# A decoder of two layers on one core: value products between the first maxima's units, and stacks loaded in six transfers

## The chip, the core and the metric

The kernel runs on one core of a Trainium2 chip. The metric is the device time of one execution in microseconds (us). The engines are named as in the profile: PE is TensorE (its clock has two levels, 1.2 and 2.4 GHz; the profile gives the granted clock as 0.50 and 1.00), DVE is VectorE, ACT is ScalarE, POOL is GpSimd, SP is SyncE, which here only issues transfers (DMAs). PE writes to PSUM, which has eight banks of 128 x 512 f32.

## The reference

Six sublayers work one after the other on x, 2048 tokens x 256 channels, each followed by a residual sum and a layer norm:

```
x = layernorm(x + self_attention_with_rope(x))            # causal, 16 heads of 16
x = layernorm(x + cross_attention(x, ctx, mask))          # ctx 1601 x 256, a mask 2048 x 1601
x = layernorm(x + quantised_linear(x))                    # fp8
x = layernorm(x + gpt_block(x))                           # causal self attention, and an MLP 256-1024-256
x = layernorm(x + cross_attention(x, ctx))                # no mask
x = layernorm(x + mixture_of_experts(x))                  # 8 experts, the best two, and a shared one
# attention: softmax(q k^T * scale [+ mask]) v, by head
```

## The kernel before

Every sublayer is a stage with a block of code for each engine; semaphores order the engines inside it. `attention_phase` is used four times: stage 1 (causal, rope, 2048 keys), stage 2 (cross, masked, 1601 keys), stage 3 (causal, biases, the mask applied by POOL's select) and stage 4 (cross, no mask, biases). The change touches this function alone.

**The front.** The projections of q and k are made in 16 pieces, `work`, each 128 channels x 512 tokens (65 for the last piece of keys in a cross stage). PE makes a piece in one of four PSUM banks (`front_bank`, banks 3 to 6); ACT and DVE cut it into three bf16 parts: `cut_high` and `cut_middle` on ACT (L397, L403), `cut_rest` and `cut_low` on DVE (L633 or L636, L643). A buffer of `SLOTS` = 4 pieces holds the parts until `store` (L207) has sent them to DRAM (`q_parts`, `k_parts`); SP stores the even pieces and POOL the odd ones. `cut_high(i)` waits until store i - 4 has landed. ACT works in the order high(i), middle(i - 1); DVE in the order rest(i), low(i - 1). After the pieces PE makes the value tiles in the same four banks, 128 keys x 256 channels each (16 in a causal stage, 13 in a cross stage), as two products each, one for each half of the contraction (L465; the profile shows two instructions for each f32 product), and ACT copies a tile to `vall` (L418, semaphore `v_kept`).

**Stacks.** For head h the bf16 parts of q and k are gathered into one of three stacks, `ks[b]` and `qs[b]` with b = h % 3, of 96 rows (`load`, L240 and L241): the combinations of parts stand as six groups of 16 rows. The semaphore `stack_in[b]` counts the transfers. SP issues `load(0)` after store 10, `load(1)` after all stores, `load(2)` after the maxima of head 0, and `load(h + 2)` once the scores of head h - 1 are all made. All transfers of SP go through its one queue, in order. Three more rows of the stack (`KQ:KM`) take the negative maxima; the key side of them is set to 1.0 once in a stage (L738).

**Units.** `unit(h, u)` is a piece of the scores of head h for the row maxima: four PE products of 32 queries x up to 512 keys side by side (L492, on the diagonal L496 too) in banks 0 to 2, which DVE reduces (L659, with mask L655). A head has 40 units in a causal stage and 64 in a cross stage. PE may be three units ahead of DVE (`unit_used`). Head 0 has all its units before any score; then come the first units of head 1 (15, 19, 15 and 24 in the four stages). When head 0's units are reduced DVE makes the maxima in six steps (`finish_max`), SP sends them to DRAM and back into the stack (`place_max`, L250 and L253, semaphore `max_in`), and PE's first `scores(0, 0)` (L516) waits for that. From then on PE mixes scores, units of the next heads and products with the values (L544), ACT does the exponentials (L426).

Before the units, DVE sets constants: L738 for three stacks, L740 to L743 for the partial maxima, the ones among the values, and O_PS. POOL adds the bias to each value tile (L342, semaphore `v_shifted`) in stages 2 to 4, and in stage 1 it prepares the masks of stage 2 (L356 to L371) all along.

PE's queue before, after the pieces:

```
                for kind, i in front:
                    if loads and (kind, i) == front[len(work) if work[0][0][0] is None else 0]:
                        pe.wait_ge(loaded, 16 * len(loads))
                    made(kind, i)
                for u in range(nu):
                    unit(0, u)
                for u in range(early_units):
                    unit(1, u)
```

## Time and profile before

| | |
|---|---|
| median of 3 runs | 3175.15 us (3171.68 to 3175.83) |
| the profiled execution | 3167.93 us, its span 3165.9 us |
| PE busy | 2958.0 us, 93% of the span |
| DVE busy | 2265.6 us, 72% |
| ACT busy | 1730.3 us, 55% |
| stage 1 | 71 to 600 us |
| stage 2 | 600 to about 1400 us |
| stage 3 | about 1495 to 2000 us |
| stage 4 | about 2120 to 2800 us |

Busy time is the time in which an instruction of that engine runs. It doesn't tell which engine holds the others up: that is read from the waits in each stretch. The times of the rows are counted from the first instruction of the profiled execution.

### The profile page before, as it was taken

To read this page: it belongs to the slowest core of one execution; us is meant where nothing else is said; L and a number is where in the kernel's file an instruction comes from. 1 tells how busy PE (TensorE), PEld (TensorE's weight loads), DVE (VectorE), ACT (ScalarE), POOL (GpSimd) and SP (SyncE) were. 2 spreads that over 40 slices of the span, in tenths; PEclk is the share of its full clock that TensorE was granted. 3 is DMA by queue.
4 is the path that set the end of the run, shared out by engine and by line. 5 is a ranking of instruction groups with operands and counts; after the bars stand their busy time and mean duration, and the time that the engine had idled before them with its cause. 6 is when DMAs were issued, how large, how long until landed. Compare 5 with 4: busy or idle time off the path is not lost. (4 is left out here: it accounts for less than half of the span.)

```text
span 3165.9 us, 97114 instructions
## 1 busy us (share of the span) xinstructions
PE 2958.0 (93%) x41235; PEld 1694.2 (54%) x41235; DVE 2265.6 (72%) x5676; ACT 1730.3 (55%) x2207; POOL 502.0 (16%) x711
## 2 busy tenths in 40 slices
PE   5999999999999999995999999999999999989994
PEld 2566666545655566552466665563333333366662
DVE  6788888587777777747788886238999999551114
ACT  2366677525556556563377777332777777722220
POOL 0255565020000000000222212202000000001113
PEclk8899999979999999996899999997999999989998
DMA  2333333310001100100311111102012211121112
GB/s 72 115 105 107 109 109 91 115 41 24 23 15 24 25 23 17 29 25 27 102 39 39 39 41 47 63 20 85 24 51 67 59 52 32 36 86 44 45 40 77
DMA packets 129376, 172.62 MB, mean 55 GB/s; under 512 B 45199, under 2 KB 99087, under 8 KB 127343
## 3 DMA queue, kind: packets, MB, share of 16 engines
q1 hardware_dynamic: 112672, 119.09, 13.8%
q0 software_dynamic: 10800, 46.76, 4.6%
q8 instruction: 327, 5.36, 0.7%
q10 hardware_dynamic: 5472, 0.56, 0.1%
q14 instruction: 105, 0.86, 0.1%
HBM read 122.76 MB, written 35.16 MB: 50 GB/s over the span
## 5 line engine op out<-in xcount | busy, mean ns | idle before, releaser
L659 DVE TENSOR_REDUCE mpart<-ps 128x1 f32<-128x512 f32 (+5 forms) x2304 | 1242.7, 587 | 146.3 <-PE ps L492 76.1
L492 PE MATMUL ps<-stack 96*32 96x401 bf16 (+5 forms) x13312 | 1261.3, 354 | 9.7 <-DVE mpart L659 5.1
L516 PE MATMUL ps<-stack 99*32 99x512 bf16 (+3 forms) x11648 | 1135.5, 369 | 40.8 <-ACT xT L426 19.3
L426 ACT ACTIVATE xT<-ps 128x1024 f32<-128x1024 f32 (+3 forms) x800 | 732.0, 938 | 439.8 <-PE ps L516 240.6
L426 ACT ACTIVATE cn<-ps 128x1024 f32<-128x1024 f32 (+4 forms) x800 | 686.2, 870 | 314.8 <-PE ps L516 161.0
L492 PEld LDWEIGHTS ps<-stack 96*32 96x32 bf16 x13312 | 491.0, 96 | 497.8 <-DVE mpart L659 231.8
L655 DVE CUSTOM_DVE_ANT_0 scrap<-ps,arena 128x401 bf16<-128x401 f32 (+1 forms) x1024 | 550.2, 574 | 150.9 <-PE ps L492 126.7
L516 PEld LDWEIGHTS ps<-stack 99*32 99x32 bf16 x11648 | 412.6, 97 | 361.7 <-issue 121.3
L544 PE MATMUL ps<-xT,vall 128*17 128x512 f32 (+4 forms) x3648 | 454.9, 504 | 1.8 <-POOL xT L379 1.0
L544 PE MATMUL ps<-cn,vall 128*17 128x512 f32 (+3 forms) x3392 | 440.8, 495 | 1.7 <-ACT cn L426 0.9
L524 PE MATMUL ps<-arena,big 128*32 128x512 fp8e4 (+1 forms) x3264 | 359.6, 382 | 0.0
L496 PE MATMUL ps<-upper,ident 128*32 128x128 bf16 x2048 | 215.8, 226 | 0.0
L544 PEld LDWEIGHTS ps<-xT,vall 128*17 128x17 f32 (+1 forms) x3648 | 133.6, 98 | 50.9 <-issue 3.3
L524 PEld LDWEIGHTS ps<-arena,big 128*32 128x32 bf16 (+1 forms) x3264 | 120.8, 98 | 54.3 <-issue 5.3
L544 PEld LDWEIGHTS ps<-cn,vall 128*17 128x17 f32 (+1 forms) x3392 | 124.9, 97 | 44.7 <-ACT cn L426 3.5
L1492 PE MATMUL ps<-arena,vall 128*128 x312 | 146.6, 593 | 0.6 <-ACT vall L1563 0.6
L1722 DVE TENSOR_TENSOR vall<-osb,ps 128x512 f32<-128x512 f32 x39 | 26.8, 688 | 146.2 <-PE ps L1492 146.2
L521 PE MATMUL ps<-lower,ident 128*32 128x128 bf16 x1024 | 120.4, 222 | 0.4 <-issue 0.4
L496 PEld LDWEIGHTS ps<-upper,ident 128*32 128x32 bf16 x2048 | 105.1, 99 | 26.1 <-issue 1.1
L994 POOL PARTITION_ALL_REDUCE small<-small x1 | 0.4, 370 | 733.0 <-issue 733.0
L1577 ACT ACTIVATE osb<-ps 128x512 f32<-128x512 f32 x39 | 23.3, 597 | 169.8 <-PE ps L1492 169.8
L360 POOL TENSOR_SCALAR arena<-wbuf 128x401 bf16<-128x401 int32 x64 | 100.4, 1569 | 78.4 <-DMA wbuf<-in_mask 74.4
(258 smaller groups left out, 2573.4 us busy)
## 6 DMA issues: line engine op xcount, KB each, us to landing
stack<-q_parts SPq DMA_DIRECT2D x384, 64.0 KB, 2.5
wbuf<-in_mask POOLq DMA_DIRECT2D x16, 800.5 KB, 5.1
stack<-k_parts SPq DMA_DIRECT2D x192, 64.0 KB, 2.6
wbuf<-in_maskT POOLq DMA_DIRECT2D x12, 1024.0 KB, 5.2
arena<-in_moe_w SPq DMA_DIRECT2D x19, 512.0 KB, 4.1
stack<-k_parts SPq DMA_DIRECT2D x192, 50.0 KB, 2.2
stack<-sums_inverse SPq DMA_DIRECT2D x16, 512.0 KB, 6.2
parts<-osb SPq DMA_DIRECT2D x240, 32.0 KB
```

The lines of the kernel that those rows point to most:

```text
L360: chain.link(nc.gpsimd.tensor_scalar(e.mask_add[:, t, a:a + n], given[:, a:a + n], 0.0, MASKED, ALU.is_equal, ALU.mult))
L426: nc.scalar.activation(e.prob[tile % P_SLOTS][0:rows, half * HALF + first:(half + 1) * HALF], S_PS(g)[0:rows, first:HALF], ACT.Exp, scale= ...
L492: last = nc.tensor.matmul(bank[quarter(j), 0:w], qs[b][0:KQ, t * P + 32 * j:t * P + 32 * j + 32], ks[b][0:KQ, a:a + w], start=True, stop=n ...
L496: last = nc.tensor.matmul(bank[quarter(j), w - P:w], e.ident16[:, quarter(j)], e.upper16, start=False, stop=True)
L516: last = nc.tensor.matmul(S_PS(g)[quarter(j), lo:hi], ks[b][0:KM, kt * P + 32 * j:kt * P + 32 * j + 32], qs[b][0:KM, half * HALF + lo:half ...
L521: last = nc.tensor.matmul(S_PS(g)[quarter(j), lo:lo + P], e.ident16[:, quarter(j)], e.lower16, start=False, stop=True)
L524: last = nc.tensor.matmul(S_PS(g)[quarter(j), lo:hi], e.big16[0:rows, quarter(j)], e.mask_one[0:rows, kt, half * HALF + lo:half * HALF + h ...
L544: last = nc.tensor.matmul(O_PS[quarter(j, HD + 1), b0 * P:CH], e.values[0:rows, kt, h, :], weights[0:rows, b0:4, j, :], start=(kt == 0), s ...
L655: nc.vector.tensor_tensor_reduce(out=e.scrap[:, g % 4, 0:w], in0=src, in1=e.mask_add[:, t, a:a + w], scale=1.0, scalar=-3.0e38, op0=ALU.ad ...
L659: nc.vector.tensor_reduce(dst, src, AX, ALU.max).then_inc(unit_used, 1)
L1492: last = nc.tensor.matmul(bank, e.pair_xT[i % 2][:, c, :], w, start=(c == 0), stop=(c == NC - 1))
L1722: nc.vector.tensor_tensor(e.pair_h[i % 2], e.gated_s[i % 2], b_bank(i), ALU.mult).then_inc(pair_h, 1)
```

## The change

Five edits in `attention_phase`:

1. After the pieces PE makes the first eight value products (four tiles, one for each bank), and spreads the others (24 in a causal stage, 18 in a cross stage) evenly between the units of head 0 and the early units of head 1.
2. DVE's constants L740 to L743 move to the beginning of the stage. The three rows of ones (L738) move from DVE to POOL, behind POOL's stores and ahead of its bias work.
3. `load` has six transfers in place of twelve, for every head: groups of 48, 32 and 16 rows, for keys and for queries. The keys of a group are one array of 16 rows, read three times or twice.
4. `load(0)` goes out behind store 8, no longer behind store 10.
5. PE waits for the biased values (`v_shifted`) at the first product with the values, no longer before the first scores.

```
                     row = 0
                     for n in (3, 2, 1):
-                        for i in range(n):
-                            sp.dma_start(ks[b][row:row + HD, 0:keys], e.kd[h, :, 3 - n, 0:keys]).then_inc(stack_in[b], 16)
-                            sp.dma_start(qs[b][row:row + HD, :], e.qd[h, :, i, :]).then_inc(stack_in[b], 16)
-                            row += HD
+                        rows = slice(row, row + n * HD)
+                        sp.dma_start(ks[b][rows, 0:keys],
+                                     e.kd[h, :, 3 - n, 0:keys].unsqueeze(0).broadcast_to([n, HD, keys])).then_inc(stack_in[b], 16)
+                        sp.dma_start(qs[b][rows, :], e.qd[h, :, 0:n, :].rearrange("d s t -> s d t")).then_inc(stack_in[b], 16)
+                        row += n * HD
...
                 for i in range(0, len(work), 2):
                     store(sp, i)
-                    if i == n_first + 2:
+                    if i == n_first:
                         stored_until(sp, n_first)
                         load(0)
...
             def _(pool):
                 for i in range(1, len(work), 2):
                     store(pool, i)
+                for b in range(3):
+                    nc.gpsimd.memset(ks[b][KQ:KM, 0:keys], 1.0).then_inc(stack_set, 1)
+                pool.wait_ge(stack_set, 3)
                 pool.wait_ge(ahead_in, 16 * len(ahead))
...
+                def value_part(t, c):
+                    (a, n), bank = k_tiles[t], front_bank(("value", t))
+                    if c == 0:
+                        bank_free(place["value", t])
+                    part = nc.tensor.matmul(bank[0:n, 0:D], v_source[:, c, a:a + n], v_weights[:, c, :],
+                                            start=(c == 0), stop=(c == NC - 1))
+                    if c == NC - 1:
+                        part.then_inc(front_made, 1)
...
-                        pe.wait_ge(stack_in[b], 192 * (h // 3 + 1))
+                        pe.wait_ge(stack_in[b], 96 * (h // 3 + 1))
...
+                    if tile == 0 and v_bias:
+                        pe.wait_ge(v_shifted, nk)
...
-                for kind, i in front:
-                    if loads and (kind, i) == front[len(work) if work[0][0][0] is None else 0]:
-                        pe.wait_ge(loaded, 16 * len(loads))
-                    made(kind, i)
-                for u in range(nu):
-                    unit(0, u)
-                for u in range(early_units):
-                    unit(1, u)
+                turned_front = work[0][0][0] is None
...
+                for i in range(len(work)):
+                    made("cut", i)
...
+                valued, all_units, first_values = 0, nu + early_units, NC * FRONT
+                while valued < first_values:
+                    value_part(valued // NC, valued % NC)
+                    valued += 1
+                for u in range(all_units):
+                    unit(u // nu, u % nu)
+                    while valued < first_values + (NC * nk - first_values) * (u + 1) // all_units:
+                        value_part(valued // NC, valued % NC)
+                        valued += 1
                 pe.wait_ge(v_kept, nk)
-                if v_bias:
-                    pe.wait_ge(v_shifted, nk)
                 pe.wait_ge(rest_made, len(work))
```

On PE, at the end of stage 1's front, the last value tiles and the first units stood like this before (`wbuf,xT` are the value weights and the source, `stack` is head 0's stack, "32x512" one of the four products of a unit):

```order
L465 MATMUL ps<-wbuf,xT 128x256 [waits v_kept_239]
L465 MATMUL ps<-wbuf,xT 128x256
L492 MATMUL ps<-stack_240 32x128 [waits stack_in0_239]
L492 MATMUL ps<-stack_240 32x128 x3
L496 MATMUL ps<-upper,ident 32x128 x4
L492 MATMUL ps<-stack_240 32x256 x4
L496 MATMUL ps<-upper,ident 32x128 x4
L492 MATMUL ps<-stack_240 32x384 x4
```

and stand like this now, the value products being L485 and the units L501:

```order
L485 MATMUL ps<-wbuf,xT 128x256 [waits rest_made_239]
L485 MATMUL ps<-wbuf,xT 128x256
L501 MATMUL ps<-stack_240 32x128 [waits stack_in0_239]
L501 MATMUL ps<-stack_240 32x128 x3
L505 MATMUL ps<-upper,ident 32x128 x4
L501 MATMUL ps<-stack_240 32x256 x4
L505 MATMUL ps<-upper,ident 32x128 x4
L501 MATMUL ps<-stack_240 32x384 x4
L505 MATMUL ps<-upper,ident 32x128 x4
L485 MATMUL ps<-wbuf,xT 128x256 [waits v_kept_239]
L501 MATMUL ps<-stack_240 32x512 [waits unit_used_239]
L501 MATMUL ps<-stack_240 32x512 x3
```

The last value product ahead of the units is now one that waits for a piece to be cut (`rest_made`), and value products stand between the units.

On SP, in the same stage, store 10 and the first stack stood like this before (L207 is a store; "x2" are stores 8 and 10):

```order
L207 DMA q_parts<-parts 384x1x512 [waits low_239,middle_239,high_239] x2
L240 DMA stack_240<-k_parts 16x2048 [waits stored2_239,stored3_239,stored1_239,stored0_239]
L241 DMA stack_240<-q_parts 16x2048
L240 DMA stack_240<-k_parts 16x2048
L241 DMA stack_240<-q_parts 16x2048
```

and stand like this now:

```order
L207 DMA q_parts<-parts 384x1x512 [waits low_239,middle_239,high_239]
L240 DMA stack_240<-k_parts 48x1x2048 [waits stored2_239,stored3_239,stored1_239,stored0_239]
L242 DMA stack_240<-q_parts 48x1x2048
L240 DMA stack_240<-k_parts 32x1x2048
L242 DMA stack_240<-q_parts 32x1x2048
L240 DMA stack_240<-k_parts 16x2048
L242 DMA stack_240<-q_parts 16x2048
L207 DMA q_parts<-parts 384x1x512 [waits low_239,middle_239,high_239]
```

Store 10 now stands behind the six transfers of the first stack, in the same queue.

On DVE the last cuts and the first units of stage 1 stood like this before:

```order
L643 TENSOR_TENSOR parts<-parts 128x512 [waits middle_239] x2
L738 MEMSET stack_240 3x2048 x3
L740 MEMSET mpart 128x64 x2
L741 MEMSET vall 128x256
L742 MEMSET mneg 128x8
L743 MEMSET ps 128x512
L659 TENSOR_REDUCE mpart<-ps 128x1 [waits unit_ready_239,parts_set_239]
```

and stand like this now, with nothing between the two:

```order
L660 TENSOR_TENSOR parts<-parts 128x512 [waits middle_239] x2
L676 TENSOR_REDUCE mpart<-ps 128x1 [waits unit_ready_239,parts_set_239]
L676 TENSOR_REDUCE mpart<-ps 128x1 [waits unit_ready_239] x39
```

## Rows read from the trace of the kernel before

**Rows 1.** The page, busy time of each engine over the span.

```profile
PE 2958.0 (93%) x41235; PEld 1694.2 (54%) x41235; DVE 2265.6 (72%) x5676; ACT 1730.3 (55%) x2207; POOL 502.0 (16%) x711
```

**Rows 2.** Timeline, PE and DVE, stage 1: start, duration; in brackets the idle time before.

```profile
104.64 11.56 PE L465 MATMUL ps<-wbuf,xT 128*128 128x256 f32 x52 [0.65 <-DVE parts L633]
...
116.55 20.84 DVE L659 TENSOR_REDUCE mpart<-ps 128x1 f32<-128x128 f32 x40 [2.73 <-PE ps L496]
...
```

**Rows 3.** Timeline, DVE, the first reduction of units in stages 2, 3 and 4.

```profile
642.94 0.58 DVE L655 CUSTOM_DVE_ANT_0 scrap<-ps,arena 128x401 bf16<-128x401 f32 x1 [1.91 <-PE ps L492]
...
1538.47 1.68 DVE L659 TENSOR_REDUCE mpart<-ps 128x1 f32<-128x128 f32 x4 [4.15 <-PE ps L496]
...
2163.12 7.31 DVE L659 TENSOR_REDUCE mpart<-ps 128x1 f32<-128x401 f32 x15 [1.84 <-PE ps L492]
```

**Rows 4.** Windows: values, units at either clock, first scores; stages 1, 2, 3, 4.

```profile
core 0: us, PE busy (x) PEld busy (x) DVE busy (x) ACT busy (x) POOL busy (x), PEclk, DMA share, GB/s
...
116.10:121.90 5.80, 4.56 (x89) 1.62 (x88) 5.35 (x12) 1.67 (x2) 0.00 (x0) 1.00 0.26 71
121.90:144.80 22.90, 21.12 (x236) 5.39 (x233) 22.87 (x50) 0.00 (x0) 0.00 (x0) 0.50 0.03 7
144.80:152.60 7.80, 7.51 (x76) 2.67 (x80) 2.67 (x6) 3.88 (x4) 5.41 (x8) 0.50 0.33 93
...
683.70:688.50 4.80, 4.80 (x52) 1.81 (x52) 1.11 (x6) 2.05 (x2) 1.74 (x3) 0.50 0.36 96
...
1566.60:1572.50 5.90, 5.60 (x56) 2.04 (x60) 2.36 (x6) 3.86 (x4) 0.59 (x2) 0.50 0.45 120
...
2205.20:2210.80 5.60, 5.32 (x56) 1.88 (x56) 2.73 (x7) 3.41 (x4) 3.38 (x5) 0.50 0.15 36
```

**Rows 5.** Timeline, ACT: `cut_high` of pieces 11 and 14 of stage 1.

```profile
94.72 0.60 ACT L397 ACTIVATE parts<-ps 128x512 bf16<-128x512 f32 x1 [0.96 <-DMA k_parts<-parts]
...
100.00 0.60 ACT L397 ACTIVATE parts<-ps 128x512 bf16<-128x512 f32 x1 [0.53 <-DMA q_parts<-parts]
...
```

**Rows 6.** Timeline, ACT: `cut_high` of piece 11 in stages 2, 3 and 4.

```profile
624.21 0.69 ACT L397 ACTIVATE parts<-ps,bcol 128x512 bf16<-128x512 f32 x1 [0.20 <-DMA k_parts<-parts]
...
1514.35 0.69 ACT L397 ACTIVATE parts<-ps,bcol 128x512 bf16<-128x512 f32 x1 [0.69 <-DMA k_parts<-parts]
...
2144.34 0.69 ACT L397 ACTIVATE parts<-ps,bcol 128x512 bf16<-128x512 f32 x1 [0.29 <-DMA k_parts<-parts]
```

**Rows 7.** DMA view, 140.2 to 143.8 us: the maxima of head 0 are stored.

```profile
DMA packets 264, 0.02 MB, mean 5 GB/s; under 512 B 264, under 2 KB 264, under 8 KB 264
...
max_parts<-mturn SPq DMA_DIRECT2D x2, 8.0 KB
```

**Rows 8.** DMA view, 680.6 to 688.5 us: a load of maxima and twelve of a stack.

```profile
q1 hardware_dynamic: 390, 0.71, 34.1%
...
stack<-q_parts SPq DMA_DIRECT2D x6, 64.0 KB, 2.2
stack<-k_parts SPq DMA_DIRECT2D x6, 50.0 KB, 2.1
stack<-max_parts SPq DMA_DIRECT2D x1, 12.0 KB
```

**Rows 9.** Windows, 584 to 589 us: large loads on all 16 DMA engines.

```profile
584.00:589.00 5.00, 5.00 (x25) 4.36 (x24) 3.93 (x20) 3.93 (x10) 0.00 (x0) 1.00 0.97 384
```

**Rows 10.** Timeline, SP and PE, stage 3: a stack's first load, its first unit.

```profile
1593.40 0.32 SPq L240 DMA_DIRECT2D stack<-k_parts  x1
...
1610.79 0.23 PE L492 MATMUL ps<-stack 96*32 96x128 bf16 x3
```

**Rows 11.** DMA view, 165 to 195 us: POOL's mask transfers beside a stack (stage 1).

```profile
q0 software_dynamic: 288, 1.87, 17.3%
```

**Rows 12.** Groups by line: the DVE memsets of L738, a POOL elementwise group.

```profile
L738 DVE MEMSET stack<- x12: 1393/1579/1765, 106.5 to 2158.6; 3x2048 bf16 x6, 3x1601 bf16 x6
...
L369 POOL TENSOR_SCALAR wbuf<-wbuf 128x512 f32<-128x512 int32 x48 | 71.4, 1487 | 63.9 <-DMA wbuf<-in_maskT 60.8
```

More of the change, by code:

```diff
@@ L454, in _, with bank_free @@
             def _(pe):
-                def made(kind, i):
-                    f = place[kind, i]
+                def bank_free(f):
                     if f >= FRONT:
@@ L460, in made @@
                         pe.wait_ge(rest_made if held_by == "cut" else v_kept, which + 1)
+                def made(kind, i):
+                    bank_free(place[kind, i])
                     bank = front_bank((kind, i))
[L462 to L478 removed]
@@ L479, in made @@
-                    last.then_inc(front_made, 1)
+                    (w, bias, src), dst, o, a, n = work[i]
+                    if w is None:
+                        for t in range(n // P):
+                            at, place_of = bank[:, t * P:(t + 1) * P], a // P + t
+                            rows = slice(place_of * 2 * D + src * D + o * P, place_of * 2 * D + src * D + (o + 1) * P)
+                            nc.tensor.matmul(at, e.rot_own[:, rows], e.ident, start=True, stop=False)
+                            last = nc.tensor.matmul(at, e.rot_added[:, 2 * place_of + src, :], e.ident, start=False, stop=True)
+                    else:
+                        for c in range(NC):
+                            last = nc.tensor.matmul(bank[:, 0:n], w[:, c, o * P:(o + 1) * P],
+                                                    src[:, c, a:a + n], start=(c == 0), stop=(c == NC - 1))
@@ L729, in _ @@
                         nc.vector.memset(ks[b][:, keys:nk * P], 1.0).then_inc(pads_set, 1)
+                for m in e.mpart:
+                    nc.vector.memset(m, -3.0e38).then_inc(parts_set, 1)
+                nc.vector.memset(e.values[:, :, :, HD], 1.0).then_inc(parts_set, 1)
+                nc.vector.memset(e.mneg[:, 3 * NT:], 0.0)
+                nc.vector.memset(O_PS, 0.0).then_inc(parts_set, 1)
                 if loads:
@@ L736, in _ @@
                 cut_low(len(work) - 1)
-                for b in range(3):
-                    nc.vector.memset(ks[b][KQ:KM, 0:keys], 1.0).then_inc(stack_set, 1)
-                for m in e.mpart:
-                    nc.vector.memset(m, -3.0e38).then_inc(parts_set, 1)
-                nc.vector.memset(e.values[:, :, :, HD], 1.0).then_inc(parts_set, 1)
-                nc.vector.memset(e.mneg[:, 3 * NT:], 0.0)
-                nc.vector.memset(O_PS, 0.0).then_inc(parts_set, 1)
                 dve.wait_ge(parts_set, 4)
```

20 lines of the change are left out of this document (4 added, 16 removed).

## The prediction

> **What bounds the kernel now.** I read the page first: PE is busy 93% of the span, DVE 72% [rows 1]. That is an average over stages, so I went on to the timeline at the seams that the change touches. In stage 1 PE makes 26 value products in 11.56 us, 0.44 us each (two instructions for each f32 product), and only then come the units of head 0; DVE reduces its 40 units in 20.84 us, 0.52 us each, with nothing between them [rows 2]. So at a stage's beginning first PE works alone with the values, then DVE is the bound and PE waits for it. The windows give PE's clock there: granted 1.00 with the values and the first 5.8 us of the units, then 0.50 for 22.9 us of units, and it is still 0.50 for the first 7.8 us of scores, where PE is the bound (7.51 us busy). The same happens in the other stages: 4.8, 5.9 and 5.6 us of scores at 0.50, with 4.80, 5.60 and 5.32 us of PE work [rows 4]. From there on PE sets the pace.
>
> So the change can pay at two places: the values may hide beneath DVE's units, and the clock may be up when the scores begin.
>
> **The value products.** PE's work in units of full clock: a causal stage has 55 units, a cross stage 83 and 88. The columns of stage 1's 55 units, counted in the code, are 26,368, which is 11 us at 2.4 GHz; rows 4 give as an upper bound 21.12 / 2 + 4.56 = 15.1 us, values among them. DVE has 28 us beside it (55 x 0.52). The 24 moved products add 24 x 0.44 = 10.6 us: 21.5 us of 28 (at most 25.7), so at 1.00 DVE stays the bound and they are hidden. In a cross stage 18 products add 7.9 us to a PE that is otherwise busy about a third of the time: hidden too. By the columns PE then works three quarters of the stretch in stages 1 and 3 (before: 11 of 28, 39%) and half of it in stages 2 and 4 (before: a third). At 0.50 a unit with its product would take PE about 0.76 us in stages 1 and 3, above DVE's 0.52, and PE would be busy all the time. In the trace the clock fell only where PE waited for DVE, and no row here shows which of these shares holds it. I take it that it stays up in the causal stages, and comes back early or stays in the others.
>
> What that gives: the scores of rows 4 at full clock save half of 7.51 + 4.80 + 5.60 + 5.32 = 23.2 us, at most 11.6; I take **10.5**. Against it, the first eight products now run before the first units and after a PE that has waited, so some of them and the first units may be at 0.50: **2** lost. Behind the last early unit stand the last product, ACT's copy of that tile and a change of ACT's work before the first exponential, where before the tiles were long done: 0.4 us in stages 1 and 3, 1.5 in 2 and 4 (there a tile's last product falls on the last unit, which DVE ends later): **4** lost.
>
> **The first stack.** Whether the units start earlier depends on how long the stack takes. `load(0)` now stands behind the issue of store 8 and waits for stores 0 to 7 to land. `cut_high(11)` waits for store 7, so it marks that time: at 94.72 in stage 1 [rows 5], at 624.21, 1514.35 and 2144.34 in the others [rows 6]. Now the stack takes six transfers of 4 KB rows. How they are laid on the 16 DMA engines the rows tell by counting. The two small transfers of maxima in one window give 264 packets, that is 2 x (128 + 4): 128 data packets and 4 that complete it [rows 7]. That store has an outer dimension of 4, its other side one of 128. A stack of twelve transfers and the load of the maxima give 390 = 12 x (16 + 16) + (3 + 3): a 16-row transfer ends in 16 completions, a 3-row one in 3 [rows 8]. So a transfer uses as many engines as its outermost dimension has in common. The new transfers have an outer dimension of 3 (against 48) and 2 (against 32), the third pair 16: three engines, two engines, sixteen. Engine 0 carries 16 + 16 + 16 + 16 + 1 + 1 = 66 rows, 270 KB in stages 1 and 3, 241 KB in 2 and 4 (keys 3.2 KB), where before it carried 12 rows.
>
> The Trainium skill says the same, in "DMA: Bandwidth & Descriptors", section "Why a DMA increments its semaphore by 16 and not by 1": the number of engines is the largest up to 16 that divides the outermost dimension of both sides; its guidelines warn that a leading broadcast of c copies keeps the transfer on c engines. The packet counts of rows 7 and 8 agree with it. Had it 16 engines, the first rival below would be the sum.
>
> An engine's rate: large loads moved 384 GB/s at a share of 0.97 of 16 engines, 24.7 GB/s for one [rows 9]. So engine 0 needs **10.9 us** (9.8 in the cross stages). The upper end comes from the stack's own transfers: 34.1% of 16 engines in 7.9 us is 43.1 engine-us for 0.71 MB [rows 8], so 270 KB take 16.4 us (14.6). To either come about 2.3 us from issue to landing, which is what a 64 KB transfer of one row per engine takes (2.2) [rows 8]. I take the lower, since that is an engine that has work all the time, as engine 0 has here.
>
> Store 10 stands behind the stack in SP's queue, and its share of 24.6 KB on engine 0 comes last: with the two stores of POOL that share the engine, 3 x 1.0 us. It lands at 94.7 + 2.3 + 10.9 + 3.0 = 110.9 in stage 1, and `cut_high(14)` waits for it, which began at 100.00 before [rows 5]. **This is the wait that takes the place of the one removed**: the first value product followed `cut_high(14)` by 4.6 us [rows 2, 5], and the unit half a us later, so units start at 116.0 against 116.55: 0.5 gained [rows 2]. Stage 3: 1514.3 + 16.2 + 5.1 = 1535.6 against 1538.47, 2.9 gained. Stage 2: 624.2 + 15.1 + 4.6 = 643.9 against 642.94, 1.0 lost; stage 4: 2144.3 + 15.1 + 4.6 = 2164.0 against 2163.12, 0.9 lost [rows 3, 6]. Sum: **1.5 gained**. With the upper rate each stage is 4.8 to 5.5 us later: some 19 lost.
>
> **The later stacks.** In stage 3 the first transfer goes out at 1593.40 and the head's first unit comes at 1610.79 [rows 10]: 17.4 us of cover against 13.2 needed, 18.7 at the upper rate. The other heads of stages 1 and 3 have 17.4 to 18.7; those of the cross stages 26 to 37, enough at either. In stage 1 POOL's mask transfers take 17.3% of 30 us of all the engines [rows 11], some 2.3 us in 13: 15.5 against 17.5, still covered, 22 at the upper rate. Six issues less on SP are nothing on the path. I take **1** lost for shared engines.
>
> **The constants.** Each memset of L738 takes DVE 1.4 to 1.8 us, three in a stage [rows 12]; they stood in DVE's queue while PE made the values, so taking them away is worth nothing by itself, and is in the start already. On POOL the lower bound is the same 1.4 us; the upper a POOL elementwise group at 1.49 us for 512 columns [rows 12], four times that for 2048: 18 us for the three. POOL's last store goes by 116, and the first maxima come into the stack at about 143 [rows 7]: the lower bound is hidden with certainty, the upper with 9 us to spare, and I count nothing. If the cover were gone (in stages 2 to 4 the bias work stands behind them), the new wait at the first product with values, not the scores, would feel it. POOL's mask work of stage 1 starts as much later; stage 2 needs it 400 us on. Constants at a stage's beginning lie where DVE waits for pieces: nothing.
>
> **Sum.** 10.5 - 2 - 4 + 1.5 - 1 = 5 to 6.5 us (the 2 and the 4 overlap in part); I take 6.5 off 3167.93, 3161.4. The profiled execution lies 7.2 us below the median of the runs, so on their scale 3168.6: **3169**.
>
> **The rivals.**
>
> *All 16 engines carry the stack.* Then it takes 2.3 us and a few for the bytes, store 10 is not held up, and the units start when the cuts end: about 10.4 us (24 products of 0.44), 8, 11.5 and 8 us earlier in the four stages, 38 together; with the warm scores 11 and the tail -4 that is 45: 3128. For it: nothing in the diff forbids it. Against it: the counts of rows 7 and 8. Chance 0.12.
>
> *The clock is the loser (slower).* With PE waiting for the stack and then for DVE, the clock drops in the first units and stays at 0.50: a unit with its product takes PE 0.76 us in stages 1 and 3 against DVE's 0.52, 0.25 x 55 = 14 us each; in stages 2 and 4 about 1.5 each; no warm scores. 31 + 4 + 1 - 1.5 = 35 longer at the worst, about 3205 to 3212. Its point of decision: the clock at the first ten units. For it: 22.9 us at 0.50 in rows 4. Against it: PE would then be busy nearly without a break, which in this trace goes with 1.00 everywhere past the first scores. Chance 0.10.
>
> *The stack becomes a head's bound (slower).* At the upper rate a load needs 18.7 us in stage 3 and 22 in stage 1 against 17.4: up to 1.3 and 4.5 us for each of 13 heads, less what PE can draw from its other work, and the 19 lost at the starts. 10 to 60 longer, about 3195. It decides where 2.3 us and 270 KB take more than 17.4, that is below 18 GB/s for an engine. For it: rows 8's own rate. Chance 0.16.
>
> *Nothing to be seen or something else*, 0.05.
>
> **How the numbers follow.** Forecast 0.57, its own range 3158 to 3180 (warm clock kept in all stages or in none: +-8; start 5 us each way). The range from 3150 to 3200 leaves out the 16 engines (0.12) and the top of the two slow rivals. 0.2% is 6.3 us, about what a measurement of this kernel can tell from no change; the forecast stands just at this bound, so of its 0.57 about 0.27 is faster, 0.25 same, 0.05 slower. Faster: with the first rival 0.39, and 0.01. Slower: 0.05 + 0.08 + 0.12. Same: the rest.
>
> **What the profile would show.** PE's granted clock 1.00 at the first scores of stages 1 and 3. `cut_high(14)` of stage 1 starting near 111, released by a store of q; first unit near 116. The six transfers in the DMA view with 10 us and more from issue to landing, where twelve took 2.2. DVE's 40 units of head 0 still in 21 us, value products between them. The forecast is wrong if a unit waits for `stack_in` past 1610 in stage 3, if `cut_high(14)` starts near 100, or if the first ten units run at 0.50 with PE without a break.

## The result and the profile after

The changed kernel takes 3208.98 us (median of 4 runs, 3206.05 to 3218.43) against 3175.49 before: 1.0113 of the time, 95% interval 1.0100 to 1.0125. It is **slower by 1.1%**, where 3169 was forecast in a range up to 3200.

The profiled execution is the slowest of the four (3218.43), 50.5 us above that of before. So the account of the trace is larger than that of the medians (33.5 us). Three places in the trace tell what happened.

*The start.* ACT's timeline in stage 1 of the changed kernel, `cut_high` of pieces 11 to 14 [rows 5]:

```profile
96.10 0.60 ACT L401 ACTIVATE parts<-ps 128x512 bf16<-128x512 f32 x1 [0.57 <-DMA k_parts<-parts]
...
98.29 0.60 ACT L401 ACTIVATE parts<-ps 128x512 bf16<-128x512 f32 x1 [1.08 <-DMA q_parts<-parts]
...
105.52 0.60 ACT L401 ACTIVATE parts<-ps 128x512 bf16<-128x512 f32 x1 [6.12 <-DMA q_parts<-parts]
...
114.43 0.60 ACT L401 ACTIVATE parts<-ps 128x512 bf16<-128x512 f32 x1 [7.79 <-DMA q_parts<-parts]
```

Piece 14 waits 7.79 us for store 10 and goes at 114.43, where it went at 100.00; piece 13 has already waited 6.12 us, for store 9 on POOL's queue. A window just before piece 14 shows what is left to do (columns as in rows 4):

```profile
110.20:114.30 4.10, 0.00 (x0) 0.00 (x0) 0.00 (x0) 0.00 (x0) 0.00 (x0) 0.50 0.13 50
```

No engine computes, and the DMA share is 0.13 at 50 GB/s: two of sixteen engines work, at 25 GB/s each, and piece 14 waits for them. Then DVE, same stage [rows 2]:

```profile
120.04 1.24 DVE L676 TENSOR_REDUCE mpart<-ps 128x1 f32<-128x128 f32 x3 [1.71 <-PE ps L505]
121.73 8.56 DVE L676 TENSOR_REDUCE mpart<-ps 128x1 f32<-128x512 f32 x16 [0.46 <-PE ps L505]
130.45 12.10 DVE L676 TENSOR_REDUCE mpart<-ps 128x1 f32<-128x512 f32 x21 [0.16 <-PE ps L501]
```

The first reduction starts at 120.04 (116.55 before), though only eight of the 32 value products are still ahead of it.

*The clock.* Windows of the changed kernel: front of values, units and early units, first scores of stage 1; then units and scores of stages 2, 3 and 4 [rows 4]:

```profile
102.80:119.50 16.70, 6.88 (x19) 4.35 (x17) 4.47 (x7) 4.68 (x10) 1.32 (x2) 0.62 0.30 109
119.50:150.70 31.20, 30.57 (x373) 13.43 (x372) 29.54 (x61) 5.03 (x14) 5.41 (x4) 0.98 0.20 62
150.70:158.50 7.80, 6.57 (x124) 3.01 (x127) 4.52 (x8) 6.76 (x7) 5.35 (x8) 1.00 0.26 74
675.40:720.70 45.30, 39.74 (x369) 13.67 (x368) 42.52 (x172) 3.86 (x11) 11.31 (x15) 0.88 0.15 41
720.70:725.50 4.80, 4.79 (x56) 1.86 (x60) 0.00 (x0) 3.30 (x3) 2.43 (x4) 0.58 0.14 57
1574.10:1605.20 31.10, 30.47 (x373) 13.37 (x376) 29.49 (x61) 5.04 (x14) 15.24 (x20) 0.99 0.20 60
1605.20:1611.10 5.90, 4.61 (x84) 2.00 (x88) 2.70 (x5) 5.05 (x6) 1.27 (x3) 1.00 0.30 85
2206.10:2250.10 44.00, 37.76 (x389) 13.29 (x388) 43.45 (x94) 3.87 (x11) 11.29 (x15) 1.00 0.15 42
2250.10:2255.70 5.60, 4.31 (x72) 1.76 (x76) 2.38 (x5) 5.02 (x5) 3.92 (x6) 1.00 0.16 59
```

The granted clock is 1.00 or nearly so through the units of stages 1, 3 and 4 and at their first scores: that part came as forecast. PE is busy 30.6 of 31.2 us in stage 1, so the values just fill it. Stage 2 is the exception: 0.88 in the units and 0.58 at the first scores.

*The later heads of stage 1.* This is where most of the time went, and no row of the start tells it. What PE and SP waited for between 200 and 550 us, before and then after (group's line, releaser, us in total, times, longest):

```profile
PE ps L516 <- DMA stack<-max_parts: 4.1, 6, 1.5
...
SPq L253 <- DMA max_parts<-mturn: 24.5, 13, 3.2
```

```profile
PE ps L525 <- DMA stack<-max_parts: 19.6, 8, 3.3
...
PE ps L501 <- DMA stack<-q_parts: 2.0, 4, 0.8
...
SPq L254 <- DMA max_parts<-mturn: 37.0, 12, 4.9
```

The units wait for their stack in four heads, but only 2.0 us in all. PE's large wait is for the maxima, and their store takes 3.1 us (37.0 / 12) where it took 1.9. Eight of the twelve heads from head 3 on stand 28 to 32 us apart, where they stood about 27, and the clock drops to 0.50 behind these waits (30.7 us between the first and the last score of stage 1, before 14.6). From head 3's units to the last score, before and then after:

```profile
197.50:571.90 374.40, 360.56 (x7788) 250.63 (x7782) 303.20 (x612) 266.23 (x358) 203.83 (x178) 1.00 0.35 104
195.40:602.20 406.80, 373.54 (x7784) 256.39 (x7779) 306.10 (x612) 266.88 (x358) 210.19 (x182) 0.96 0.34 96
```

PE is busy 13.0 us longer, at a mean clock of 0.96, and idle 19.4 us longer: together 32.4 us.

Why the maxima are late is seen at single heads. From the issue of their store (L251) to the issue of their load back (L254), in the changed kernel, one head beside a mask transfer of POOL and one without:

```profile
256.94 1.19 SPq L251 DMA_DIRECT2D max_parts<-mturn  x2
257.31 0.60 POOL L360 DMA_DIRECT2D wbuf<-in_mask  x1 [0.30 <-POOL arena L375]
261.93 0.24 SPq L254 DMA_DIRECT2D stack<-max_parts  x1
...
341.81 1.19 SPq L251 DMA_DIRECT2D max_parts<-mturn  x2
344.40 0.24 SPq L254 DMA_DIRECT2D stack<-max_parts  x1
```

5.0 us against 2.6. The DMA view of 256.9 to 261.9 us (q0 is POOL's queue, q1 SP's):

```profile
q0 software_dynamic: 144, 0.82, 46.3%
q1 hardware_dynamic: 264, 0.02, 3.6%
```

SP's 264 packets are those of the two small stores alone [rows 7]: no stack is under way, and what the maxima wait for is POOL's mask. In eight heads of the changed kernel's stage 1 a mask transfer goes out between 1.0 us ahead of the store and 0.5 us behind it, and the store takes 4.9 to 6.2 us. In the kernel before none does: there the mask went out 1.4 to 3.6 us ahead in 13 heads, and the store took 2.5 to 4.3 us in all. The few engines of the stack come in one step earlier. The time to landing of POOL's `in_maskT` transfers, before and then after:

```profile
DMA to landing us min/median/max: 5.1/5.2/6.6
...
DMA to landing us min/median/max: 5.1/7.3/12.4
```

It is up to 12.4 us when the transfer goes out beside a stack. So POOL's round of two transfers and its arithmetic grows from 26 to 28 us to mostly 30 and more, longer than a head needs undisturbed (26.3), and the maxima's store keeps running into the next mask. That the rounds fall into step like this is read from the times; no run moved one against the other. Stage 3 has the same structure without POOL's mask transfers, and loses nothing there.

The account, from the starts of the same instructions in the two traces (us after less before):

| | stage 1 | 2 | 3 | 4 | sum |
|---|---|---|---|---|---|
| `cut_high(11)` to first unit | +2.0 | +3.4 | -0.3 | +4.2 | +9.3 |
| first unit to first score | +2.5 | +4.0 | +2.5 | +1.4 | +10.4 |
| first scores (stage 1: to head 3's units; others: to the last score) | -8.0 | -0.1 | -1.7 | -1.4 | -11.2 |
| stage 1, head 3's units to the last score | +32.4 | | | | +32.4 |
| up to piece 11 of each stage, and behind stage 4 | | | | | +8.6 |

Of the last line's 8.6 us, 6.1 lie behind the last score of stage 4, in code that is the same. The pieces 0 to 11, beside which the moved constants now stand, take as long as before in each stage, within 0.3 us.

### The profile page after: what moved, and what is told of

Same layout as the page of the kernel before. It is cut to its first block and busy times, and to the rows that moved or that the text cites. A ratio compares the mean times of both kernels' runs of the same rounds, so it can differ in the third digit from the quotient of the medians.

```text
span 3215.5 us, 96728 instructions
## 1 busy us (share of the span) xinstructions
PE 2942.3 (92%) x41234; PEld 1708.1 (53%) x41235; DVE 2251.7 (70%) x5664; ACT 1730.4 (54%) x2207; POOL 521.9 (16%) x723
## 3 DMA queue, kind: packets, MB, share of 16 engines
q1 hardware_dynamic: 103072, 119.05, 12.7%
## 5 line engine op out<-in xcount | busy, mean ns | idle before, releaser
L501 PE MATMUL ps<-stack 96*32 96x401 bf16 (+5 forms) x13312 | 1225.7, 343 | 14.0 <-DVE mpart L676 3.3
L525 PE MATMUL ps<-stack 99*32 99x512 bf16 (+3 forms) x11648 | 1142.0, 370 | 59.5 <-DMA stack<-max_parts 25.1
L501 PEld LDWEIGHTS ps<-stack 96*32 96x32 bf16 x13312 | 495.2, 96 | 465.5 <-DVE mpart L676 204.1
L525 PEld LDWEIGHTS ps<-stack 99*32 99x32 bf16 x11648 | 420.7, 97 | 375.8 <-issue 116.4
L364 POOL TENSOR_SCALAR arena<-wbuf 128x401 bf16<-128x401 int32 x64 | 100.5, 1570 | 102.2 <-DMA wbuf<-in_mask 98.3
```

The lines of the kernel that those rows point to most:

```text
L364: chain.link(nc.gpsimd.tensor_scalar(e.mask_add[:, t, a:a + n], given[:, a:a + n], 0.0, MASKED, ALU.is_equal, ALU.mult))
L501: last = nc.tensor.matmul(bank[quarter(j), 0:w], qs[b][0:KQ, t * P + 32 * j:t * P + 32 * j + 32], ks[b][0:KQ, a:a + w], start=True, stop=n ...
L525: last = nc.tensor.matmul(S_PS(g)[quarter(j), lo:hi], ks[b][0:KM, kt * P + 32 * j:kt * P + 32 * j + 32], qs[b][0:KM, half * HALF + lo:half ...
```

## The experiments

Theory 1: the transfers whose outermost dimension is 3 or 2 run on three or two DMA engines, which holds store 10 back at each start and, beside POOL's masks, the stacks and maxima of stage 1's heads. Theory 2: the loss lies in the values between the units, or in the place of `load(0)`. The runs form three groups, four rows of the table each, and each group has its own chip; the kernel before took 3152.77, 3167.62 and 3170.26 us there, so each ratio is to the kernel before on the same chip.

| run | median us (range) | to before (95%) |
|---|---|---|
| after_twelve | 3146.69 (3134.61 to 3164.97) | 0.9978 (0.9956 to 1.0000) |
| after_depth | 3135.78 (3121.23 to 3149.43) | 0.9950 (0.9931 to 0.9970) |
| before_six | 3216.74 (3216.10 to 3225.85) | 1.0204 (1.0187 to 1.0221) |
| after_store10 | 3209.06 (3185.45 to 3229.60) | 1.0155 (1.0115 to 1.0195) |
| before_again | 3167.00 (one run) | |
| first_depth | 3189.84 (3157.61 to 3197.17) | 1.0067 (1.0046 to 1.0088) |
| depth_values_ahead | 3176.40 (3171.93 to 3180.72) | 1.0026 (1.0016 to 1.0036) |
| depth_store10 | 3171.52 (3152.03 to 3174.07) | 1.0007 (0.9992 to 1.0022) |
| cross_ahead | 3159.70 (3144.70 to 3166.48) | 0.9955 (0.9938 to 0.9971) |
| cross_dense | 3143.21 (3134.93 to 3147.35) | 0.9910 (0.9894 to 0.9927) |
| after_thin_masks | 3185.81 (one run) | |
| depth_constants | 3204.51 (one run) | |

What the traces of these runs say of the places in question (us; "st." is the stage; the last column is the time from the first to the last score):

| kernel | cut 14, st. 1 | first unit, st. 1 | first unit to first score, st. 1 / 2 / 3 / 4 | scores, st. 1 |
|---|---|---|---|---|
| before | 100.0 | 116.1 | 28.7 / 41.3 / 28.6 / 42.6 | 427.1 |
| after | 114.4 | 119.5 | 31.2 / 45.3 / 31.1 / 44.0 | 451.5 |
| after_twelve | 105.8 | 110.7 | 30.7 / 45.8 / 30.8 / 58.9 | 427.2 |
| after_depth | 103.6 | 107.2 | 30.7 / 45.1 / 30.8 / 44.0 | 423.1 |
| before_six | 100.5 | 124.5 | 28.6 / 41.3 / 28.7 / 42.6 | 471.2 |
| after_store10 | 100.8 | 116.3 | 32.8 / 57.0 / 34.1 / 58.8 | 465.9 |
| before_again | 101.2 | 117.0 | 28.6 / 41.3 / 28.6 / 42.6 | 426.6 |
| first_depth | 102.8 | 106.4 | 30.7 / 45.1 / 31.7 / 44.1 | 441.3 |
| depth_values_ahead | 104.2 | 118.3 | 28.6 / 41.3 / 28.6 / 42.5 | 428.5 |
| depth_store10 | 100.3 | 107.0 | 30.7 / 56.9 / 35.9 / 58.7 | 419.1 |
| cross_ahead | 103.0 | 106.6 | 30.7 / 41.3 / 30.8 / 42.5 | 426.6 |
| cross_dense | 104.0 | 107.7 | 30.7 / 42.8 / 30.9 / 45.4 | 425.1 |
| after_thin_masks | 113.9 | 119.0 | 31.0 / 56.1 / 31.8 / 44.0 | 414.0 |
| depth_constants | 104.2 | 107.9 | 40.1 / 61.4 / 45.8 / 62.5 | 420.0 |

**after_twelve** puts the twelve transfers of 16 rows back into the changed kernel (and 192 for 96 in the wait).

> The changed kernel, but a stack in twelve transfers of 16 rows as before (all 16 engines by the completions). Theory 1, the few engines: store 10 is no longer held, cut_high(14) of stage 1 starts near 99 (114.43 in the changed kernel), the units start near 107, the heads of stage 1 go on at 27 us each; about 8 us gained at each of four starts, 11 for the warm first scores and the 30 of stage 1's heads back: 3125 to 3140. Theory 2, the values between the units or the order of queues cost the time: 3190 or more.

The gain over the changed kernel is there, 1.4% by the ratios, and the direction is theory 1's: units at 110.7, stage 1's heads back at 427.2. The size is not: 3125 to 3140 was expected, and `cut_high(14)` at 105.8 is still 5.8 us late, since SP issues the twelve transfers of the stack from 95.37 to 101.06 and store 10 only at 101.17. Stage 4 shows a new thing: 58.9 us from the first unit to the first score, all at 0.50. Its window, from the first unit on:

```profile
2149.90:2208.00 58.10, 57.50 (x385) 17.41 (x376) 44.70 (x94) 3.26 (x9) 10.79 (x15) 0.50 0.13 34
```

PE is busy 57.50 of 58.10 us: at half clock a unit with its share of the values takes longer than DVE needs. And the clock does not come back for it, though PE has hardly a pause.

**after_depth** keeps six transfers and changes only the order of the rows inside a group, so that the head's 16 dimensions are outermost on the DRAM side. Keys and queries are ordered alike, so the products are the same sums.

```diff
-e.kd[h, :, 3 - n, 0:keys].unsqueeze(0).broadcast_to([n, HD, keys])
+e.kd[h, :, 3 - n, 0:keys].unsqueeze(1).broadcast_to([HD, n, keys])
-e.qd[h, :, 0:n, :].rearrange("d s t -> s d t")
+e.qd[h, :, 0:n, :]
```

> The changed kernel with six transfers whose outermost dimension is the head's 16 dimensions on the DRAM side (row order inside a group: dimension, then part) and the 48, 32 or 16 rows of the stack on the other. Theory 1: 16 divides both, 16 engines carry them, so as with twelve transfers, 3120 to 3140. Theory 2 (six transfers are slow for their size, not for their outermost dimension, or the loss is elsewhere): about 3205.

3135.78, 0.9950: faster than before by 0.5%, and 1.6% below the changed kernel by the ratios, for the same bytes in the same six transfers. This is the run that isolates the outermost dimension.

The Trainium skill's rule in "DMA: Bandwidth & Descriptors", section "Why a DMA increments its semaphore by 16 and not by 1", gives 16 engines for 16 against 48, 32 or 16 rows. The trace agrees: in stage 3, from 1595.4 to 1599.0 us with a stack under way, the DMA share is 0.93 at 190 GB/s, and the transfers of 192 KB land in 3.6 and 4.0 us. The cuts in its stage 1:

```profile
102.07 0.60 ACT L401 ACTIVATE parts<-ps 128x512 bf16<-128x512 f32 x1 [3.31 <-DMA q_parts<-parts]
...
103.58 0.60 ACT L401 ACTIVATE parts<-ps 128x512 bf16<-128x512 f32 x1 [0.40 <-DMA q_parts<-parts]
```

Piece 14 goes at 103.58, and the first unit at 107.2, 12 us before the changed kernel's. Its clock through the units of stages 1, 2 and 4:

```profile
107.20:137.90 30.70, 30.09 (x369) 13.22 (x368) 29.66 (x62) 5.29 (x16) 6.01 (x4) 1.00 0.31 82
623.60:668.70 45.10, 38.85 (x373) 13.59 (x372) 42.53 (x172) 3.89 (x11) 12.34 (x16) 0.90 0.24 55
2132.00:2176.00 44.00, 37.78 (x393) 13.33 (x396) 43.43 (x94) 3.95 (x11) 12.12 (x16) 1.00 0.23 55
```

**before_six** has the six transfers of the change in the kernel before, and nothing else.

> The kernel before with nothing but the six transfers of the change. Theory 1: stage 1's heads 1.5 to 2.5 us longer each, since a stack lands 19 us after its issue beside the masks' transfers, and each start 2 to 5 us later: 3205 to 3225. Theory 2: 3170 to 3180.

1.0204: the six transfers alone cost more than the whole change did. First unit of stage 1 at 124.5, 8.4 us late; first to last score of stage 1 471.2 against 427.1. The unit does not wait for the stack itself. With the stack behind store 10, the next victim is store 11 on POOL's queue: piece 15 waits 7.07 us for it, the values start that much later, and they end only with the first unit.

```profile
108.70 0.60 ACT L398 ACTIVATE parts<-ps 128x512 bf16<-128x512 f32 x1 [7.07 <-DMA q_parts<-parts]
...
110.08 14.51 PE L466 MATMUL ps<-wbuf,xT 128*128 128x256 f32 x52 [5.22 <-DVE parts L634]
```

Theory 2 has nothing to say here, as values and order are those of before. In stage 1's heads PE waited 35.9 us for maxima and for no stack. The `in_mask` transfers, which now go out beside the stack, land in 8.5 us in the median (5.1 before), and 14 of the 16 stores of the maxima take 5.0 us and more:

```profile
wbuf<-in_mask POOLq DMA_DIRECT2D x16, 800.5 KB, 8.5
```

**after_store10** moves `load(0)` behind store 10 in the changed kernel.

```diff
-                    if i == n_first:
+                    if i == n_first + 2:
```

> The changed kernel with load(0) behind store 10 again. If only the few engines matter, the units wait for the stack itself in place of store 10: starts within 3 us of the changed kernel, 3200 to 3215. If the place ahead of store 10 is what costs, cut_high(14) is back near 100 and the units follow it: 3175 to 3190.

The ratio, 1.0155, is no better than the changed kernel's 1.0113, as theory 1 has it. `cut_high(14)` is back at 100.8, but the units start at 116.3, 3.2 us ahead of the changed kernel's: piece 15 now waits 7.26 us for store 11, and the first unit 3.66 us for its stack. The trace loses more elsewhere: the units and first scores of stages 2 and 4 ran at 0.50, and stage 1's heads took 465.9 us.

**before_again** is the kernel before, for a trace from the second chip.

> The kernel before, unchanged, for a trace from the chip on which these runs are made. Either theory: the milestones of stages 1 to 4 as in the first trace (slast of stage 4 within 10 us), and if the chip differs, a shorter time behind stage 4 (about 394 us, as in the other runs, where the first trace has 409).

Its milestones lie within 3.4 us of the first trace's in all four stages. The time behind stage 4 is 410.6 us, as in the first trace (409.5); the 394 us were of the chip of the first four runs. So the tail differs by 15 us between chips, and only ratios on one chip are compared here.

**first_depth** gives the first stack alone the 16 engines (`if h == 0`).

> The changed kernel, in which the first stack alone goes on 16 engines (rows ordered by dimension, then part); the stacks of heads 1 to 15 go as in the changed kernel. Theory 1 (two separate losses by the few engines: store 10 held at the starts, and stage 1's heads beside the masks): starts as in the run with 16 engines (units of stage 1 at 107 to 110, cut_high(14) below 106), and stage 1 from its first score to its last 450 us and more, against 423 with 16 engines: 3155 to 3170 on this chip. Rival: the loss in stage 1's heads follows from the late start alone; then 3136.

The two losses are separate: the starts are those of after_depth (units at 106.4), while stage 1's heads take 441.3 us against 423.1. The trace's 18 us are less than the 27 expected, but the trace is of the fastest of its five runs (3157.61); the median lies 32 us higher, at 1.0067, and what the longer runs spent it on no trace shows.

**depth_values_ahead** is after_depth with all value products ahead of the units (`first_values = NC * nk`).

> Stacks on 16 engines as in the run with the rows ordered by dimension, load(0) behind store 8, but all value products ahead of the units, as before the change. Theory A (values between units pay): about 10 us later units in stages 1 and 3, clock 0.50 for 20 us in each stage's units and in the first scores; some 15 to 25 us slower than with values between, 3150 to 3160. Theory B (what they save the clock takes back: units and values at 0.50 hold each other up in stages 2 and 4, 57 us for 44): runs spread by less than 10 us, and the median within 10 us of 3136.

Slower than the kernel before by 0.26%, and 0.8% above after_depth by the ratios: theory A. The spread is small, 9 us, as theory B had it. So both hold: values between the units pay on the whole (0.8%), and the spread is smaller without them. The units start at 118.3, later than before, although the stack was there long since: without this edit an early stack is worth nothing, as the values then set the start.

**depth_store10** is after_depth with `load(0)` behind store 10.

> As the run with the rows ordered by dimension, but load(0) behind store 10 (edit 4 undone). If edit 4 helps once the stack has 16 engines: the first unit waits for the stack, 3 us later in each stage, 12 us in all: 3148. If the cuts set the start: within 4 us of 3136.

First unit of stage 1 at 107.0 against 107.2: the place of `load(0)` changes nothing at this start (from piece 11 to the first unit, the other stages differ by -1.1 to +1.6 us). The run is 0.6% above after_depth all the same; in its trace both cross stages fell into the half clock. The windows of stage 4, the values ahead and then the units:

```profile
2136.00:2145.80 9.80, 6.86 (x26) 3.88 (x25) 5.38 (x10) 5.37 (x12) 1.66 (x3) 1.00 0.91 275
2145.80:2204.50 58.70, 57.71 (x393) 17.63 (x393) 44.72 (x94) 3.92 (x12) 12.87 (x16) 0.50 0.16 38
```

The clock was 1.00 when the units began, and fell with them. In the profiles with `load(0)` behind store 10 this happened in four of four cross stages, with it behind store 8, the constants early and the values spread over all units in two of ten. Whether the place has a part in that, or chance, stays open.

**cross_ahead** keeps the values between the units in the causal stages only (`NC * (FRONT if nu == 40 else nk)`).

> Stacks on 16 engines, load(0) behind store 8, and values between the units in the causal stages only; in the cross stages all value products stand ahead of the units. Theory B (in the cross stages units and values at 0.50 hold each other up, 57 us for 44, in some runs; in the causal stages the values between keep the clock at 1.00): first unit to first score 41.3 us in stages 2 and 4 in every run, 30.7 in 1 and 3; 0.7% below the kernel before, with a spread under 10 us. If the spread came from elsewhere (stage 1's heads, the chip), it stays at 25 us and more.

The stretches came as expected, 30.7 / 41.3 / 30.8 / 42.5, and the ratio is 0.9955, where 0.993 was expected. The spread is 22 us, 9 without the two fastest of nine runs: not under 10, so the cross stages were not its only source.

**cross_dense** has one value product after every second unit in the cross stages, until all are made.

```diff
+                spread = all_units if nu == 40 else 2 * (NC * nk - first_values)
-                    while valued < first_values + (NC * nk - first_values) * (u + 1) // all_units:
+                    while valued < first_values + (NC * nk - first_values) * min(u + 1, spread) // spread:
```

> As the run before it, but in the cross stages one value product after every second unit, so that the 18 are done after 36 units. If PE's share of the stretch decides on its clock: 1.00 through these 36 units, then 0.50 with DVE as the bound, 42 us from first unit to first score; 0.9% below the kernel before, spread under 12 us. If the clock falls at the first units all the same: 50 us and more from first unit to first score in stages 2 and 4 in some runs, and a spread of 20 us.

**The fastest: 0.9910 (0.9894 to 0.9927)**, with a spread of 12 us, about as the first of the two expectations has it. The windows of stage 4, the units with values and those without:

```profile
2132.10:2154.00 21.90, 21.57 (x201) 7.96 (x200) 20.23 (x39) 5.01 (x11) 11.92 (x16) 0.96 0.29 65
2154.00:2177.50 23.50, 21.98 (x196) 5.31 (x196) 23.46 (x54) 0.11 (x1) 0.00 (x0) 0.58 0.14 32
```

With a product to every second unit PE is busy 21.57 of 21.90 us at 0.96; the clock falls behind the last product, when DVE is the bound (busy 23.46 of 23.50 us). The two stretches, 42.8 and 45.4 us, are still 1.5 and 2.8 us longer than before the change. Against cross_ahead, on the same chip, the gain is in the start: from piece 11 to the first unit 12.7 and 13.5 us in stages 2 and 4, where it was 20.7 and 22.1. Against after_depth the traces show no gain in the stretches (45.1 and 44.0 there); that its median ratio is 0.4% lower comes from runs without a trace.

**after_thin_masks** leaves POOL's mask transfers of stage 1 in number, but cuts all except the first two to 8 columns; the masks are then all open, so stage 2 computes without its mask.

> The changed kernel, in which POOL's mask transfers of stage 1 but the first two bring 8 columns in place of 1601 and 2048; the masks then are all open, so stage 2 computes without its mask. POOL's arithmetic, the order and the number of transfers stay. Theory 1 (few engines beside the masks' traffic): stage 1 from first to last score 420 to 427 us (451.5 in the changed kernel), first scores still at 150 since store 10 is still held. Rival (the stacks on few engines are too slow by themselves): 440 and more.

Stage 1 from first to last score: 414.0, against 451.5. SP's and PE's waits between 200 and 550 us:

```profile
SPq L254 <- DMA max_parts<-mturn: 20.3, 14, 1.9
...
PE ps L527 <- DMA stack<-max_parts: 0.6, 2, 0.3
```

The store of the maxima takes 1.5 us (20.3 / 14), and PE waits for them 0.6 us and for a stack not at all. The stacks still go on few engines here. Beside after_depth (423.1) this says that the loss in stage 1's heads needs both: few engines, and POOL's megabytes. How much the kernel before would gain by thin masks was not run; it had 4.1 us of such waits. This is a single run, and it also shows stage 2 at half clock (56.1 us).

**depth_constants** is after_depth with the constants and the rows of ones set by DVE behind the last cut.

> Stacks on 16 engines, load(0) behind store 8, values between units, but the constants and the three rows of ones set by DVE behind the last cut, as before (edit 2 undone). Their 8 us on DVE then lie between the last cut and the first reduction: with the values no longer ahead of the units, first reduction 5 to 8 us later in each stage than with edit 2 (stage 1: 113 to 115 against 107.6), 20 to 30 us in all, unless the cuts' end was not the last wait.

DVE's timeline in its stage 1:

```profile
108.61 1.76 DVE L752 MEMSET stack<- 3x2048 bf16 x1 [0.48 <-issue]
110.75 1.76 DVE L752 MEMSET stack<- 3x2048 bf16 x1 [0.38 <-issue]
112.89 1.76 DVE L752 MEMSET stack<- 3x2048 bf16 x1 [0.38 <-issue]
114.73 0.19 DVE L754 MEMSET mpart<- 128x64 f32 x2
115.10 0.27 DVE L755 MEMSET vall<- 128x256 f32 x1 [0.19 <-issue]
115.31 0.07 DVE L756 MEMSET mneg<- 128x8 uint32 x1
115.49 0.48 DVE L757 MEMSET ps<- 128x512 f32 x1
116.00 1.09 DVE L673 TENSOR_REDUCE mpart<-ps 128x1 f32<-128x128 f32 x3
```

The first reduction starts at 116.00; with edit 2 it started at 107.63. So the constants cost 8.4 us in stage 1 once the values are no longer their cover; 5 to 8 was expected. PE, which waits through them, then has the clock at 0.50 for 10 to 62 us of each stretch; the single run's 3204.51 holds both.

## Why the prediction was wrong

**The step that failed: "1 lost for shared engines", in the paragraph on the later stacks.** Measured, the heads of stage 1 lost 32.4 us in the profiled execution, the largest of the errors. The prediction asked only whether a stack lands before its own head's first unit, and there it was nearly right: "still covered, 15.5 against 17.5", with a first unit 17.5 to 20.2 us after the stack's first transfer from head 3 on and 2.0 us of waits in four heads. What it put at nothing, without a reason, is what a stack on few engines does to others: it holds up POOL's mask transfers (up to 12.4 us for 5.2), these then meet the stores of the maxima (4.9 to 6.2 us for 2.5 to 4.3), and from head 3's units on PE waits for the maxima 25.1 us where it waited 4.1, and runs at half clock behind these waits. I spread POOL's mask traffic as a mean share over the time (17.3%), but it comes in bursts of 0.8 and 1.0 MB of about 5 us. The runs show it: after_thin_masks (414.0 for 451.5), before_six (471.2 for 427.1) and after_depth (423.1). The rival with a chance of 0.16, a head bound by its stack, has the right place and, with 10 to 60 us, the right size for stage 1, but not the mechanism; in stage 3 the 17.4 us held.

**The start, mis-sized.** The mechanism was right: three and two engines, store 10 behind them, `cut_high(14)` late, the unit 5.1 us behind it. 1.5 us gained was the forecast, 9.3 lost the measurement. From the issue of the stack to `cut_high(14)` it took 18.3, 16.2, 18.2 and 16.9 us, where 16.2, 15.1, 16.2 and 15.1 were worked out. That is 1 to 2 us more than the sum had by the lower of its two times for the bytes (10.9 and 16.4 us in stage 1), and less than by the upper one. These are 7 of the 10.8 us. Another 1.8 lie in the comparison: the sum's time is that of the first unit, and it was set against the first reduction of before, 0.4 to 0.5 us later.

**The values between the units, mis-sized.** 2 + 4 us lost was the forecast, 10.4 came. In stage 4 it came as forecast (1.4 for 1.5); stages 1 and 3 lost 2.5 each, where PE is the bound (30.6 of 31.2 us busy), and stage 2 4.0, with 11.1 us at half clock. PE's work was underestimated: by the columns PE would work half of a cross stretch, in the windows it is busy 37.8 of 44.0 us at full clock. At half clock the stretch takes 57 to 59 us, where it was 41.3 and 42.6 before: so my "about 1.5 each" for the cross stages, in the rival with the cold clock, should have been about 16 each, as after_twelve, after_store10 and depth_store10 show. And a PE busy without a break did not bring 1.00 back, which I had held against this rival.

**The warm first scores, right in sum, partly by luck.** 10.5 us forecast, 11.2 measured. But stage 1 gave 8.0 where half of 7.51 was counted, because before the change the clock also fell behind a later wait, from 176.5 to 183.3 us, which the prediction did not look at ("the clock fell only where PE waited for DVE"); stage 2 gave 0.1 for 2.4, since its clock did not stay up; stages 3 and 4 gave 1.7 and 1.4 for 2.8 and 2.7.

**The constants, right with their condition.** The trace shows no cost at their new place. depth_constants shows the price without that cover, 8.4 us in stage 1, so edit 2 is what lets the others pay.

**The sum.** The terms of the forecast give 5.0 us gained (6.5 was taken for an overlap that did not show). With 10.8 worse for the start, 4.4 for the units and 31.4 for the later stacks (32.4 for 1), and 0.7 better for the scores, it is 40.9 us lost; the other 8.6 us of the trace's 49.6 lie outside the places counted, and the median lies 9.5 below the profiled execution.

**The rival with 16 engines** can be priced by after_depth: 0.5% gained, some 16 us, where 45 was worked out. The starts came nearly as it had them (units earlier by 9.3, 5.7, 11.7 and 5.5 us after piece 11), but the stretches up to the first score were longer by 9.4 us in all, and its runs differ by 28 us.

What stays open: why the runs of the changed kernels with values between the units differ by 12 to 44 us, where those of before differ by 8 to 14 on a chip. The cross stages at half clock (12 to 15 us each above full clock) explain a part; cross_ahead has 22 us without them. A candidate is stage 1, where a head takes 26.3 us or about 30, by whether a mask meets its maxima; no run tested it. And why the place of `load(0)` and the half clock went together.

## What to carry to other kernels

Count the DMA engines of a transfer before merging it with others: the six transfers with an outermost dimension of 3 and 2 made 1.0113 of the time before, the same six with 16 outermost 0.9950. A transfer on few engines is not slow for its own waiter alone: a store of POOL's queue beside it waited 6 us and a mask transfer took twice its time, and a third transfer, small and on the critical path, can be hit by that in turn. So when a term is only a mean share of the DMA engines, look for the bursts, and for which small transfer they can meet. Where products are to fill PE between units that wait for another engine, placing them densely (one to every second unit) was the best of the variants tried: spread thin, they ran at half clock in some stretches and made PE the bound.

## What the runs showed of the hardware

- PE's clock stayed at 0.50 for 58.7 us while PE was busy 57.7 of them (depth_store10, stage 4), and stayed at 1.00 in the same code with 37.8 of 44.0 us busy (after_depth). What decides between the two, these runs don't tell.
- A stack on few engines in SP's queue delays transfers of POOL's queue: ACT waited 7.07 us for store 11 in before_six, and 6.12 us for store 9 in the changed kernel, 3.31 us with the stack on 16 engines and 0.71 us in the kernel before, where the stack went out behind store 10; a mask transfer of 1 MB landed in up to 12.4 us, where it took 5.2.
- With two of sixteen DMA engines at work, the core's DMA moved 50 GB/s (changed kernel, 110.2 to 114.3 us).
- From the issue of two stores of 8 KB to the load that waits for their landing took 2.6 us with no other transfer under way, and 4.9 to 6.2 us when a mask transfer of 0.8 or 1.0 MB went out between 1.0 us ahead and 0.5 us behind.
- The same code behind stage 4 took 394 us on one chip (four traces, within 0.6) and 409 to 416 us on the others.
